# Second attention of a two-layer kernel: q and k normalised straight out of PSUM, their roots by Ln and Exp, the identity added to the output weights, and the steps of a batch and of the opening laid in a new order

## The reference, cut to what matters

```python
def _rms_norm(x, g):
    y = x * rsqrt(mean(x * x, axis=-1, keepdims=True) + 1e-6)
    return y * g
xn = _rms_norm(x, g_norm) * (1.0 + scale) + shift      # scale, shift of the batch
q, k, v = heads(xn @ W_qkv)                            # 16 heads of 32
q = _rms_norm(q, g_q)                                  # over the 32 of a head
k = _rms_norm(k, g_k)
attn = softmax(einsum('bhqd,bhkd->bhqk', q, k) * 32 ** -0.5)
o = concat_heads(attn @ v)                             # (8, 256, 512)
return o + o @ W_out
```

## Time and profile before

| | us |
|---|---|
| time, median of 3 runs (1952.59 to 1955.15) | 1954.99 |
| span of the profiled execution, first to last instruction | 1947.8 |
| first load of the second attention's x to its first projection | 838.6 to 858.5 |
| opening, first projection to first transposed scores of batch 0 | 858.5 to 938.85 |
| slots of batches 0 to 7 | 938.85 to 1339.25 |
| tail of the second attention | 1339.25 to 1362.55 |
| experts of the second layer, to the end | 1362.55 to 1947.8 |

### The profile page before, as it was taken

The page is one execution under the profiler, slowest core; times in us unless marked ns, Lnnn a source line. Parts: engine busy times, 40 slices in busy tenths (PEclk is TensorE's granted clock), DMA queues, the critical chain, the costliest instruction groups (busy, mean ns, idle before and its releaser), DMA issues. The chain is left out here.

```text
span 1947.8 us, 31517 instructions
## 1 busy us (share of the span) xinstructions
PE 1643.8 (84%) x10250; PEld 958.6 (49%) x10250; DVE 1092.5 (56%) x2038; ACT 563.0 (29%) x1061; POOL 266.3 (14%) x344
## 2 busy tenths in 40 slices
PE   5788888888478999936777888887999999999998
PEld 1122232332154555512344444444777777778776
DVE  4455555555456445344456556653565666665665
ACT  0333434334234223123434333332122112111211
POOL 4211110110532222221111100110000000000000
PEclk7799999999679999966889889988899999999999
DMA  5422211210699999551122101120940000000000
GB/s 164 149 61 61 61 28 32 60 44 12 224 286 179 218 199 239 99 184 33 33 45 44 44 17 38 34 49 18 165 89 1 11 11 0 11 11 0 11 11 12
DMA packets 195487, 145.42 MB, mean 75 GB/s; under 512 B 126492, under 2 KB 163120, under 8 KB 195336
## 3 DMA queue, kind: packets, MB, share of 16 engines
q1 hardware_dynamic: 179000, 109.84, 22.2%
q0 software_dynamic: 15632, 34.30, 8.1%
q10 hardware_dynamic: 768, 0.13, 0.0%
HBM read 50.95 MB, written 41.56 MB: 47 GB/s over the span
## 5 line engine op out<-in xcount | busy, mean ns | idle before, releaser
L1889 PE MATMUL d_bank<-XTh,d_wgu 128*128 (+1 forms) x1408 | 245.6, 273 | 0.0
L1977 ACT ACTIVATE d_SG<-d_bank 128x256 f32<-128x256 f32 x264 | 101.4, 384 | 398.0 <-PE d_bank L1889 311.9
L330 DVE TENSOR_REDUCE W<-a_bn 128x1 f32<-128x512 f32 x256 | 163.6, 685 | 87.0 <-PE a_bn L244 83.5
L2039 DVE SCALAR_TENSOR_TENSOR d_HF<-d_bank,d_SG 128x256 f32<-128x256 f32 x264 | 112.0, 424 | 164.5 <-ACT d_SG L1977 146.2
L1889 PE MATMUL d_bank<-XTl,d_wgu 128*128 (+1 forms) x704 | 192.3, 273 | 0.0
L312 ACT ACTIVATE W<-a_bt 128x512 f32<-128x512 f32 x256 | 144.1, 596 | 151.7 <-PE a_bt L263 151.3
L1889 PEld LDWEIGHTS d_bank<-XTh,d_wgu 128*128 128x128 f16 x1408 | 138.1, 98 | 17.6
L281 PE MATMUL a_bc<-W 128*64 128x512 f32 x512 | 142.9, 637 | 0.0
L244 PE MATMUL a_bn<-W 97*128 97x512 f16 x256 | 100.6, 426 | 47.1 <-DVE W L330 28.1
L2046 DVE TENSOR_TENSOR d_H_l<-d_HF,d_H_h 128x256 f16<-128x256 f32 x264 | 112.4, 426 | 9.2 <-DVE d_H_h L2044 0.2
L263 PE MATMUL a_bt<-W 98*128 98x512 f16 x256 | 92.1, 389 | 20.1 <-ACT W L312 17.5
(11 more groups left out here) (287 smaller groups left out, 3017.1 us busy)
## 6 DMA issues: line engine op xcount, KB each, us to landing
W<-W SPq DMA_DIRECT2D x96, 64.0 KB, 2.9
W<-W POOLq DMA_DIRECT2D x96, 64.0 KB, 2.6
W<-in_x SPq DMA_DIRECT2D x8, 512.0 KB, 3.9
W<-W SPq DMA_DIRECT2D x32, 128.0 KB
x<-x_rows SPq DMA_DIRECT2D x8, 512.0 KB, 10.0
c_a_A<-c_H SPq DMA_DIRECT2D x64, 64.0 KB, 3.0
c_a_B<-c_H POOLq DMA_DIRECT2D x64, 64.0 KB, 2.8
c_a_CT<-c_a_CS SPq DMA_DIRECT2D x32, 128.0 KB
```

Source lines behind the costliest of these rows:

```text
L330: self.nc.vector.tensor_reduce(self.NM[:, s * cols:(s + 1) * cols], self.bn[s % 2][:, :].rearrange("p (k n) -> p k n", k=cols), AX, ALU.ma ...
L1889: mm = MM(b[:, w * CH:(w + 1) * CH], wgu[:, f, w, KF * s + k, :], X[m][:, k, toks], start=(w == 0 and k == 0 and i == 0), stop=(k == KF - ...
L1977: nc.scalar.activation(SG[k % 3][:, :], GU[(f + 3) % 4][:, 0:CH], ACT.Silu, scale=1.0 / WS).then_inc(silu, 1)
L2039: V.scalar_tensor_tensor(out=HF[:, :], in0=b[:, CH:2 * CH], scalar=1.0 / WS, in1=SG[k % 3][:, :], op0=ALU.mult, op1=ALU.mult).then_inc(mul ...
```

## The change

- `norm(j)`, j = 0 to 3 for q0, q1, k0, k1, takes the place of the takes, `norm` and `scale`: ACT squares a projection straight from PSUM (512 columns), DVE sums it over heads (16 sums), ACT takes Ln and then Exp with scale -0.5, DVE makes one Newton step in three instructions of 16 columns, and DVE multiplies PSUM by the root into QK. The bank is let go only then. Sqrt and reciprocal are gone; the same is done to the roots of x's rows. A preload names the table set that holds both Ln and Exp.
- The identity is added once to W_out (DVE, four 128 x 128 blocks) ahead of its split. `out` becomes `out0` and `out1`; ACT makes XTh and DVE XTl from PSUM, in one instruction each. `post_done` is given after spread.
- The order of a batch: lag 4, last nat at slot 14, head to slot 12, `xs` ahead of `first`, v0 at slot 0, out0 at slot 8, out1 at slot 11, qk0 at 10, qk1 at 13.
- The opening: nat 0 to 15 of batch 0 in four groups between the projections of batch 1; the squares of x in pieces (`near`, `far1` to `far3`).

```diff
@@ Core.plan @@
-        parts = [("first",)], []
+        parts = [*((m,) for m in before), ("first",)], []
+        span = (self.slots if last_nat is None else last_nat + 1) - self.lag
-            after.setdefault(self.lag + j * (self.slots - self.lag) // self.slots, []).append(("nat", j))
+            after.setdefault(self.lag + j * span // self.slots, []).append(("nat", j))
@@ layer1_attention @@
-        plan = c.plan(7, {0: ("xs",), 1: ("recip",), 2: ("spread",), 5: ("xt0", "xt1", "out"), 7: ("q0",), 8: ("k0",),
...
+        plan = c.plan(13, {0: ("v0",), 1: ("xt0", "xt1", "recip"), 2: ("xm0", "xm1", "xn0", "xn1"), 3: ("spread",),
+                           4: ("q0",), 5: ("q1", "sq0", "rt0", "nm0"), 6: ("k0", "sq1", "rt1", "nm1"), 7: ("k1", "sq2", "rt2", "nm2"),
+                           8: ("out0", "sq3", "rt3", "nm3"), 9: ("high0", "low0"), 10: ("qk0",), 11: ("out1", "qh0", "ql0"),
+                           12: ("high1", "low1"), 13: ("qk1",), 14: ("qh1", "ql1")},
+                      ("shift", "v1"), last_nat=14, before=("xs",))
+        begin = [(0, names("var0 xs xt0 xt1 xm0 xm1 xn0 xn1 q0 q1 sq0 rt0 nm0 k0 near sq1 rt1 nm1 k1 sq2 rt2 nm2 sq3 rt3 nm3 v0 "
+                           "qk0 qh0 ql0 qk1 qh1 ql1 v1")),
+                 (1, names("xs xt0 xt1 far1 xm0 xm1 xn0 xn1")), (0, nats(0)), (1, names("q0 sq0 rt0")), (0, nats(1)),
+                 (1, names("nm0 q1 far2 sq1 rt1")), (0, nats(2)), (1, names("nm1 k0 far3 sq2 rt2")), (0, nats(3)),
+                 (1, names("nm2 k1 last sq3 rt3 nm3")), (0, names("shift")), (1, names("qk0 qh0 ql0 qk1 qh1 ql1 all_set var2"))]
@@ tensor @@
-                    pe.wait_ge(qn_done, n.idx + 1)
+                    pe.wait_ge(qn_done, 4 * n.idx + 2 * w + 2)
@@ scalar @@
+                nc.scalar.preload_act_table_set("natural_log_exp_and_others")
-                    nc.scalar.activation(SQ[:, t, :, :], QK[:, t, :, :], ACT.Square).then_inc(sq_done, 1)
-                    nc.scalar.activation(ssq[:, :], ssq[:, :], ACT.Sqrt).then_inc(std_done, 1)
+                    nc.scalar.activation(SQ[:, j % 2, :], bank[:, :], ACT.Square).then_inc(sq_done, 1)
+                    act.wait_ge(sum_done, 4 * n.idx + j + 1)
+                    nc.scalar.activation(root[:, j, :], ssq[:, j, :], ACT.Ln, bias=eps[:, 0:1]).then_inc(log_done, 1)
+                    act.wait_ge(log_done, 4 * n.idx + j + 1)
+                    nc.scalar.activation(root[:, j, :], root[:, j, :], ACT.Exp, scale=-0.5).then_inc(root_done, 1)
+                    nc.scalar.activation(g.XTh[:, 2 * u:2 * u + 2, bass.ds(n.idx * S0, S0)],
+                                         bank[:, :].rearrange("p (k s) -> p k s", k=2), ACT.Copy,
+                                         scale=1.0 / WS).then_inc(x_high, 1)
@@ vector @@
+                    for k in range(KF):
+                        ins = V.tensor_tensor(ws[3][:, k, k * P:(k + 1) * P], ws[3][:, k, k * P:(k + 1) * P], g.ident[:, :], ALU.add)
-                    V.tensor_scalar(QK[:, t, w, :], bank[:, :], 1.0 / WS, None, ALU.mult).then_inc(qk_out, 1)
-                    chain.did(V.tensor_scalar(ssq[:, :], ssq[:, :], 1.0 / D, EPS, ALU.mult, ALU.add))
-                    V.reciprocal(ssq[:, :], ssq[:, :]).then_inc(var_done, 1)
-                    V.tensor_tensor(qk, qk, ssq[:, :].unsqueeze(2).to_broadcast([P, 64, D]), ALU.mult).then_inc(qn_done, 1)
+                    V.tensor_reduce(ssq[:, j, :], heads(SQ[:, t, :]), AX, ALU.add).then_inc(sum_done, 1)
+                    dve.wait_ge(root_done, 4 * n.idx + j + 1)
+                    chain.did(V.scalar_tensor_tensor(out=h, in0=y, scalar=-0.5, in1=y, op0=ALU.mult, op1=ALU.mult))
+                    chain.wait(dve)
+                    chain.did(V.scalar_tensor_tensor(out=h, in0=ssq[:, j, :], scalar=eps[:, 0:1], in1=h, op0=ALU.add, op1=ALU.mult))
+                    chain.wait(dve)
+                    chain.did(V.scalar_tensor_tensor(out=y, in0=h, scalar=1.5, in1=y, op0=ALU.add, op1=ALU.mult))
+                    chain.wait(dve)
+                    V.tensor_tensor(heads(QK[:, t, w, :]), heads(bank[:, :]),
+                                    root[:, j, :].unsqueeze(2).to_broadcast([P, c.heads, D]), ALU.mult).then_inc(qn_done, 1)
+                    dve.wait_ge(qn_done, 4 * n.idx + j + 1)
+                    dve.sem_inc(a.proj_out, 1)
-                        chain.did(V.scalar_tensor_tensor(out=a.CT[:, ks, :], in0=ps, scalar=1.0 / WS, in1=a.CT[:, ks, :],
-                        chain.did(V.tensor_copy(hi, a.CT[:, ks, :]))
-                        chain.did(V.tensor_tensor(lo, a.CT[:, ks, :], hi, ALU.subtract))
+                    chain.did(V.scalar_tensor_tensor(out=g.XTl[at], in0=bank[:, :].rearrange("p (k s) -> p k s", k=2),
+                                                     scalar=1.0 / WS, in1=g.XTh[at], op0=ALU.mult, op1=ALU.subtract))
```

More of the change, by code:

```diff
@@ L109, in __init__ @@
         self.n_early = n_early
[L110 removed]
+        self.base0 = 2 * n_pre + v_opening * n_v + 1 + n_early + n_ahead
         self.uses = n_pre + n_v + 1 + n_post
@@ L137, in walk @@
 def walk(plan, table, b=None, b1=None, b2=None, last=None):
-    batch = {"first": b, "slot": b, "route": b, "rank": b, "place": b, "expert0": b, "expert1": last, "nat": b1, "shift": b1, "recip": last, "spread": last, "out": last, "rows": last, "logit": last}
+    batch = {"first": b, "slot": b, "route": b, "rank": b, "place": b, "expert0": b, "expert1": last, "nat": b1, "shift": b1, "recip": last, "spread": last, "out": last, "rows": last, "logit": last,
+             "out0": last, "out1": last, "high0": last, "high1": last, "low0": last, "low1": last}
     for name, *args in plan:
@@ L361, in prime, with batches @@
         dve.sem_inc(self.post_done, 1)
-def batches(eng, c, plan, pre, values, table, opening, closing=None, ahead=False):
+def batches(eng, c, plan, pre, values, table, opening, closing=None, ahead=False, begin=None,
+            final=("expert1", "recip", "spread", "rows", "out", "logit")):
     head, rest = plan
@@ L369, in batches @@
     b0, b1 = Batch(0, 0), Batch(0, 1)
[L370 to L373, removed]
+    if begin:
+        for n, steps in begin:
+            walk(steps, opening, b1=(b0, b1)[n], b2=(b0, b1)[n])
+    else:
+        walk([(m,) for m in pre + values] + [("others",)], opening, b1=b0, b2=b0)
+        walk([("nat", s) for s in range(c.slots)] + [("shift",)], opening, b1=b0)
+        walk([("all_set",)], opening, b2=b0)
+        walk([(m,) for m in pre], opening, b2=b1)
     walk(head, opening, b0, b1, Batch(1, 0) if ahead else None)
@@ L393, in batches @@
     walk(closing[1], steps, end, None, None)
-    walk([("expert1",), ("recip",), ("spread",), ("rows",), ("out",), ("logit",)], steps, last=end)
+    walk([(m,) for m in final], steps, last=end)
 class Chain:
@@ L1489, in pre_qk, with out @@
                         mm.then_inc(a.proj_made, 1)
-                def out(n, uses):
+                def out(n, uses, u):
                     pe.wait_ge(a.ctx_norm, 2 * (n.idx + 1))
[L1493 to L1502, removed]
+                    bank = a.pe_take(pe, uses)
+                    for dd in range(2):
+                        d = 2 * u + dd
+                        for k in range(KF):
+                            for m, (ws, xs) in enumerate(((woh, CH), (woh, CL), (wol, CH))):
+                                mm = nc.tensor.matmul(bank[:, dd * S0:(dd + 1) * S0], ws[:, k, d * P:(d + 1) * P],
+                                                      xs[:, k, :], start=(k == 0 and m == 0),
+                                                      stop=(k == KF - 1 and m == 2))
+                    mm.then_inc(a.proj_made, 1)
                 def table(uses):
@@ L1509, in table @@
                              "qk0": lambda n: pre_qk(n, uses, 0), "qk1": lambda n: pre_qk(n, uses, 1),
-                             "spread": lambda n: a.pe_spread(pe, n, uses), "out": lambda n: out(n, uses)}
+                             "spread": lambda n: a.pe_spread(pe, n, uses),
+                             "out0": lambda n: out(n, uses, 0), "out1": lambda n: out(n, uses, 1)}
                     for t in range(2):
@@ L1729, in table @@
                              "recip": lambda n: a.dve_recip(dve, n), "spread": lambda n: spread(n, uses, chain),
-                             "out": lambda n: out(n, uses, chain)}
+                             "low0": lambda n: low_rows(n, uses, chain, 0), "low1": lambda n: low_rows(n, uses, chain, 1)}
+                    for j in range(4):
+                        steps[f"nm{j}"] = lambda n, j=j: norm(n, uses, chain, j)
                     for t in range(2):
-                        for j, name in enumerate("qk"):
-                            steps[f"{name}{t}"] = lambda n, t=t, j=j: take_qk(n, uses, t, j)
```

174 lines of the change are left out of this document (96 added, 78 removed).

## The result

The changed kernel takes 1924.7 us (median of 4 runs, 1920.04 to 1926.34) where the one before, on the same chip, takes 1953.79 (4 runs): the medians differ by 29.1 us, and the ratio of the runs is 0.986, interval 0.9845 to 0.9875, which is 27 us. The forecast was 1919, range 1902 to 1940. The profiled execution took 1924.49 us with a span of 1922.8, so 1.7 us lie around a span. The span of before was 1947.8: spans fell by 25.0, where the forecast sum was 36.

A forecast was written before the change was run, and what follows sets the result against it. No engine is full, PE is nearest; chains, waits and slow clock bound the kernel. Opening 10, batch 0 6.3, batches 1 to 5 19, batch 6 0.5, tail 0.3 sum to 36: span 1912, plus 7.2 is 1919 us, range 1902 to 1940.

The forecast's parts named there:

- Rivals A and B: Norm chain is the bound: 1937 us, chance 0.20; buffer A is late and PE's clock falls: 1933 us, chance 0.12.
- The shift costs nothing: In a batch, the shift's DMA lands 1.8 us after issue and v1 covers 2.6, so PE does not wait.
- Rival C: Ln and Exp exchange tables, two loads of 1.28 us in every norm, 82 us in all: 1995 us, chance 0.04.
- Rival D: Denser PE keeps the clock up, 2.3 us more in each of six batches, better opening: 1902 us, chance 0.14.
- rival E: Waits return in slots 3, 11 and 13, half the opening's gain stays: 1945 to 1958 us, chance 0.06.
- Batch 0 from its first Exp: Without spread and out, it takes 46.3 us where it took 52.6: gain 6.3 us (2 to 10).
- Batches 1 to 5: Second attention: a batch falls from 57.8 to 54.0 us, gain 3.8 each, 19 in five.
- Batch 6: It has no norm; nat 0 waits some 3 us for A, the rest is shorter: 35.1 us against 35.6.
- The opening's own terms: Low half of k done 2.7 us sooner; first nat to first Exp 36.2 us instead of 44.5; 10 taken.
- the slow clock of a batch: PE's slowed matmuls cost about 2.7 us a batch before, and 2.3 was left for the new order.
- pipeline ends: Some 2.2 us of a batch of 57.8 that PE's counted waits don't include.
- The walk: Three engine queues followed through a batch at full clock: 42.5 us of work plus 9.2 of waits, 51.7.

The follow-up runs named there:

- e6: Changed kernel with Sqrt in place of Ln in the four norms of a batch, so q and k become zero; 1977.81 us.
- e4: Changed kernel with 16 needless matmuls of 256 columns put into PE's 2.06 us wait at slot 3; 1907.94 us.
- e3: Changed kernel with both opening and batches in the order of before, so only the steps themselves are new; 1950.63 us.
- e5: Changed kernel with the second pair of modulations moved from slot 2 to slot 3, behind Exp 3; 1913.53 us.
- e10: Changed kernel with 16 needless matmuls of 256 columns at slot 0, where PE has no wait to fill; 1940.64 us.
- e2: Changed kernel with the steps of a batch in the order of before, opening and single steps as changed; 1940.11 us.
- e11: Kernel before with only the roots made by Ln and Exp, table set preloaded, no Newton step, order and norm as before; 1948.05 us.

## Why the prediction was right, and where its size was off

**Right: mechanism and order of sizes.** No table load in a batch; norm 1.3 us from sum to multiplication; first Exp at 931.5 (near 930); maxima 1.7 us in five batches (under 1 each); 2.06 us for Exp behind the modulations (1.9 forecast), 1.5 before out1 (1.6), 0.61 to 0.66 at slot 13 (0.9), 1.19 before the last product (1.3); clock 0.93. Rivals A and B did not come: projections wait 0.9 us for banks in five batches, and A is late only once, 2.13 us in batch 6, not at slot 4 of every batch as I had it (0.7). "The shift costs nothing" did not hold in two batches (0.92 and 1.68). Rival C lost with the single load at 838.62: as the Trainium skill, "ScalarE: Activation LUTs", "Table sets: the hidden batching unit", has it, one set held both here; in e6, once Sqrt had been in between, each of the two got a load. Rival D's clock did not come by itself; e4 shows that it was there to be had. The time of rival E, little of it left, is that of the steps without the order (e3).

**The sum by stretch**, forecast gain first, then by spans: opening 10, 9.6. Batch 0 from its first Exp 6.3, 5.2. Batches 1 to 5 19, 11.9 (288.91 - 277.04). Batch 6 0.5, -0.4: its wait for A. Batch 7 and tail 0.3, -0.3. The experts, 0 forecast, -1.0 (585.25 to 586.27); not followed up. Sum 36 and 25. The opening's own terms held: 35.4 us from first projection to first nat, 2.7 less as forecast, and 36.9 on to the first Exp, for 36.2.

**The term that failed is the slow clock of a batch.** I had 57.8 as 42.5 of work, 10.3 of waits, "2.7 of slow clock, and some 2.2 of pipeline ends". The table gives 43.3 of work with its ends, 10.5 of waits and 3.9 of slow clock. So 1.2 us that I took for pipeline ends, and let shrink with the waits (12.5 to 9.2), were slow clock. And for the new order I left 2.3, where 3.8 stayed. The walk itself held: 42.5 + 9.2 = 51.7 at full clock, and the batch with a clock of 1.00 (e4) has 51.4. With 3.8 in place of 2.3 the forecast batch would have been 55.5; it is 55.2, or 55.4 from first scores to first scores. That the loss stayed at 3.8 although waits fell by 2.6 explains the whole gap of 7 us over five batches: the waits moved, and a single one of 2.06 does as much to the clock as the many before. e4, e5 and e10 show this cause, each from another side. Less 1.1 in batch 0 has the same sign, but no run isolates it.

**The base was off the other way.** I took 7.2 us around the span, the difference of a median of runs to one profiled span. All the other profiled executions here have their own time 1.7 to 1.9 above the span. The one of before was by this estimate near 1949.5, under all four of its other runs. This made the forecast 5.5 us too high, the sum made it 11 too low; the two left 6. That 1919 came so near to 1924.7 is in part this luck.

**What stays open.** The clock loss varies between kernels with the same waits: e2 and e3 both have 10.0 us of waits a batch, but 3.9 and 5.2 of loss, and e11 has 0.9 less of waits than before and 1.0 more of loss. By the runs I can't say how long a slow stretch will be. In the changed kernel all five start behind the long wait, in e5 some start only in q0, and e11 has one, at 1112, with only the waits of 0.55 and 0.49 us next ahead of it. That the filled gap keeps the clock is shown; what else makes it fall is not. So e11 and e3 may have hidden a small gain in the clock's share; no run separates it.

## What to carry to other kernels

Add PE's waits and its busy time over a stretch and compare the busy time with what the same instructions take at full clock: the difference is what the slow clock costs. Here a batch with one wait of 2 us lost nearly 4 more that way. Before new steps go into an engine's in-order queue, look which Exp (or other step that PE needs) stands behind them: here relieving DVE alone moved the waits to ACT and gained nothing, and in the batches only steps and order together gained. Where a wait can't be removed, try to shorten it, or to fill it: both paid here, and the same filler in a place without a wait cost its full length.

## What the runs showed of the hardware that was not expected

- Needless matmuls made the kernel faster: 16 of 256 columns, 1.91 us a batch, in a wait of 2.06 us took the 3.8 us of slow clock in a batch away, 17 us in all; at slot 0 they cost 16 us.
- In the changed kernel the wait of about 2 us was followed in all five batches by 2.5 to 3.8 us for spread's eight matmuls instead of 1.99. Behind one of 1.15 us or less (e5) they took 1.99 in three batches and 2.60 and 3.00 in the others, and 2.2 of the 3.8 us of loss stayed.
- The same instructions behind the same waits can run at either level: the product at 1112.85 in e11 took 1.98 us, the one at 1115.34 in before 1.08.
- A table load placed in front of an instruction that waits for another engine is hidden: in e6 the load at 1083.81 ended 0.98 us before its activation could start.
- Ln and Exp side by side took no load in the changed kernel and one each in e6, where Sqrt had been in use.
- Ln on 16 columns with a bias from memory takes 0.31 us, Exp without it 0.21; Ln without it, on 12 columns, takes 0.21 too.
